# Routed rows that carry the gates of all eight experts

## The chip, the cores and the metric

The kernel runs on one core of one Trainium2 chip. The metric is the device time of one execution in microseconds, taken as the median of several runs. TensorE (PE) does the matrix products, VectorE (DVE), ScalarE (ACT) and GpSimd (POOL) the element-wise work; SyncE (SP), ACT and POOL have queues from which DMAs are issued.

## What is computed

A pre-norm transformer layer over x of 16 batches x 512 tokens x 256 features: banded attention with 16 heads, then a mixture of eight experts of which each token uses two.

```python
x = x + attention(layernorm(x))                  # banded softmax attention
gating = softmax(X @ Wg + bg)                    # X = layernorm(x), 8 gates for each token
top = argsort(gating)[..., -2:]                  # the two experts of each token
h = silu((X @ W1[e] + b1[e]) * (X @ W3[e] + b3[e]))
expert_out = h @ W2[e] + b2[e]
mixed = sum over the two experts of gating[e] * expert_out[e]
x = x + mixed @ Wf + bf                          # Wf is folded into W2 ahead of time
```

## The kernel before

The program has three parts, each a block that all engines leave before the next begins: a setup, the attention with the routing, and the experts.

**Attention and routing** (`build_attention`). A batch is 512 tokens, four tiles of 128. The work is a software pipeline of steps i = -1 to 17, each of 16 rounds n; the order on every engine is written out by hand, and step i holds rounds of attention of batch i, projections of batch i+3, the second norm of batch i-1, and the choice of experts of batch i-2. In each round PE writes scores for a maximum into `p_max`, DVE reduces them (L977), and PE's next scores wait for that.

For batch b the routing goes as follows. DVE normalises x2 to `x2n` (L930), ACT writes its high half into the row tile `rows[b % 3]` (`high_rows`, L829), POOL the low half (`low_rows`, L728). A row is 2 x 256 fp16 words and META = 6 words: token number, first gate, second gate, two words each (L41 to L45). DVE forms the eight gates (`softmax_gates`, L1031 to L1037), takes the largest and its expert, lowers that gate by 2 in place and takes the next (`choose`, L1039 to L1057); `place` (L1059 to L1075) turns PE's running counts into row numbers `slots`. POOL's `note(b)` (L684 to L693) copies the token number and the two gates into the row's words. POOL's `scatter(b, j)` (L695 to L707) sends the four tiles of rows to the regions of their j-th experts in the DRAM tensor `routed`, four indirect DMAs for j = 0 and four for j = 1. An expert reads one gate, the first of the row: so between the two sets POOL waits until the four DMAs of the first set have read the rows, and copies the second gate over the first (L699 to L704).

The order on POOL in a step is: `split_qk(i+2, 3)`, `low_rows(i-2)`, in even steps `all_magnitudes` (L712), in odd steps `low_weights(..., 2)` (L716), `scatter(i-3, 0)`, `split_qk(i+3, 0)` (L682), `second_norm` (L670), `note(i-2)`, `residual_bias` (L720), `split_qk(i+3, 1)`, `norm(i+4)`, `split_qk(i+3, 2)`, `scatter(i-3, 1)`, and in even steps `low_weights(..., 0)` and `(..., 1)`. For the last three batches (PROMPT = 13) both sets of batch i-2 go out at the end of step i, one behind the other. POOL leaves the block when all scatters have landed. SP meanwhile fills the end of the first expert's region (`fill`, L170) once DVE has the table of counts (`expert_tables`, L1077).

**Experts** (`build_experts`). For each expert a loop over tiles of 256 routed rows: SP loads the rows transposed (L1465), DVE copies them into place (L1579), PE does 48 matmuls of `hidden` and 24 of `result` (L1491, L1503), ACT loads the rows' words (`load_words`, L1539), and in `weighted` (L1541 to L1548) copies the token numbers and scales the result by the gate; POOL adds the scaled rows into `out` by an indirect DMA (L1628). In this trace there are 68 tiles.

Of the kernel before, what the change touches and what calls it, by code (L numbers as in the profile page):

```python
# [37 lines left out]
KC = HID // P  # L38
TOKENS = B * S
REGION = TOKENS + FILL  # L40
META = 6  # L41

M_TOKEN, M_GATE, M_SECOND = 0, 2, 4
USED = 4
ROW = 2 * D + META  # L45
NOWHERE = 1 << 20
NEG = -1e30
# [425 lines left out]
def build_attention(nc, io, keep):  # L473
    with ExitStack() as ctx:  # L474
# [31 lines left out]
        mv2 = sb("mv2", [P, NT, 2])  # L506
        rs2, var2 = sb("rs2", [P, NT]), sb("var2", [P, NT])
        lg, ge, gates = sb("lg", [P, NT, NE]), sb("ge", [P, NT, NE]), sb("gates", [P, NT, NE])
        gm, gs = sb("gm", [P, NT]), sb("gs", [P, NT])
        gw = [sb(f"gw{j}", [P, NT]) for j in range(TOPK)]  # L510
        one = [sb(f"one{j}", [P, NT, NE]) for j in range(TOPK)]
# [154 lines left out]
        @block.gpsimd  # L666
        def _(pool):
            def rstd(var, rs):

                return nc.gpsimd.tensor_tensor(rs[:], var[:], keep["neg_half"][:], ALU.pow)  # L670

            def norm(b):
                pool.wait_ge(s_mv1, b + 1)
                wait(pool, s_xn, b)
                rstd(var1, rs1)
                pool.drain()
                nc.gpsimd.tensor_tensor(shift1[:], less1[:], rs1[:], ALU.mult).then_inc(s_rs1, 1)

            def split_qk(b, k):

                taken(pool, s_free, "QK", b, k)
                nc.gpsimd.tensor_tensor(qk_lo[:, k, :], qf[:, k, :], qk_hi[:, k, :], ALU.subtract).then_inc(s_qk, 1)  # L682

            def note(b):  # L684

                words = rows[b % 3][:, :, 2 * D:ROW]
                pool.wait_ge(s_ch, b + 1)
                nc.gpsimd.tensor_copy(words[:, :, M_TOKEN:M_TOKEN + 2].bitcast(I32)[:, :, 0], keep["token"][:])
                nc.gpsimd.tensor_copy(words[:, :, M_GATE:M_GATE + 2].bitcast(F32)[:, :, 0], gw[0][:])
                nc.gpsimd.tensor_copy(words[:, :, M_SECOND:M_SECOND + 2].bitcast(F32)[:, :, 0], gw[1][:]).then_inc(s_noted, 1)  # L690
                pool.drain()
                nc.gpsimd.tensor_scalar(keep["token"][:], keep["token"][:], float(S), 0.0, ALU.add, ALU.add)
                pool.drain()  # L693

            def scatter(b, j):  # L695

                if j == 0:
                    pool.wait_ge(s_placed, b + 1)
                if j:  # L699
                    words = rows[b % 3][:, :, 2 * D:ROW]  # L700
                    pool.wait_ge(s_scat[b % 3], 128 * (b // 3) + 64)
                    nc.gpsimd.tensor_copy(words[:, :, M_GATE:M_GATE + 2].bitcast(F32)[:, :, 0],
                                          words[:, :, M_SECOND:M_SECOND + 2].bitcast(F32)[:, :, 0])
                    pool.drain()  # L704
                for t in range(NT):
                    nc.gpsimd.indirect_dma_start(out=io["routed"], out_offset=bass.IndirectOffsetOnAxis(  # L706
                        ap=slots[b % 3][:, j, t:t + 1], axis=0), in_=rows[b % 3][:, t, :].bitcast(U16), in_offset=None).then_inc(s_scat[b % 3], 16)  # L707

            def all_magnitudes(e):

                pool.wait_ge(s_wsum, e + 1)
                nc.gpsimd.tensor_tensor(w_all[:], w_sum[:], keep["half"][:], ALU.pow).then_inc(s_wall, 1)  # L712

            def low_weights(e, k):
                pool.wait_ge(s_whi, 3 * e + k + 1)
                nc.gpsimd.tensor_tensor(w_lo[:, k, :], w_mat[:, k, :], w_hi[:, k, :], ALU.subtract).then_inc(s_wlo, 1)  # L716

            def residual_bias(b):
                pool.wait_ge(s_xn, b + 1)
                nc.gpsimd.tensor_tensor(xt[b % HELD][:], xt[b % HELD][:], keep["bfc_row"][:, None, :].to_broadcast([P, NT, D]), ALU.add).then_inc(s_res, 1)  # L720

            def second_norm(b):
                pool.wait_ge(s_mv2, b + 1)
                rstd(var2, rs2).then_inc(s_rs2, 1)

            def low_rows(b):
                pool.wait_ge(s_hi2, b + 1)
                nc.gpsimd.tensor_tensor(rows[b % 3][:, :, D:2 * D], x2n[:], rows[b % 3][:, :, 0:D], ALU.subtract).then_inc(s_lo2, 1)  # L728

            for b in range(LEAD_BATCHES):  # L730
                norm(b)
                for k in range(4):
                    split_qk(b, k)
            norm(2)
            for i in STEPS:
                if exists(i + 2) and i > FIRST_STEP:
                    split_qk(i + 2, 3)
                if exists(i - 2):
                    low_rows(i - 2)
                if split_expert(i) is not None:  # L740
                    all_magnitudes(split_expert(i))
                if stored_expert(i) is not None:
                    low_weights(stored_expert(i), 2)
                if exists(i - 3) and i - 3 < PROMPT:
                    scatter(i - 3, 0)
                if exists(i + 3):
                    split_qk(i + 3, 0)
                if exists(i - 1):
                    second_norm(i - 1)
                if exists(i - 2):  # L750
                    note(i - 2)
                if exists(i):
                    residual_bias(i)
                if exists(i + 3):
                    split_qk(i + 3, 1)
                if exists(i + 4):
                    norm(i + 4)
                if exists(i + 3):
                    split_qk(i + 3, 2)
                if exists(i - 3) and i - 3 < PROMPT:  # L760
                    scatter(i - 3, 1)
                if exists(i - 2) and i - 2 >= PROMPT:
                    for j in range(TOPK):
                        scatter(i - 2, j)
                if split_expert(i) is not None:
                    low_weights(split_expert(i), 0)
                    low_weights(split_expert(i), 1)
            for p in range(3):
                pool.wait_ge(s_scat[p], 16 * TOPK * NT * len(range(p, B, 3)))
# [142 lines left out]
        def _(dve):  # L912
# [118 lines left out]
            def softmax_gates(b):  # L1031
                dve.wait_ge(s_ge, b + 1)
                nc.vector.tensor_reduce(out=gs[:], in_=ge[:], axis=AX.X, op=ALU.add)
                dve.drain()
                nc.vector.reciprocal(gs[:], gs[:])
                dve.drain()
                nc.vector.tensor_tensor(gates[:], ge[:], over_experts(gs), ALU.mult)  # L1037

            def choose(b, j):  # L1039

                dve.drain()
                if j == 0:
                    wait(dve, s_noted, b)
                nc.vector.tensor_reduce(out=gw[j][:], in_=gates[:], axis=AX.X, op=ALU.max)
                dve.drain()
                nc.vector.tensor_tensor(one[j][:], gates[:], over_experts(gw[j]), ALU.is_ge)
                dve.drain()
                nc.vector.tensor_tensor(pick[:], one[j][:], keep["expert_row"][:, None, :].to_broadcast([P, NT, NE]), ALU.mult)
                dve.drain()
# [2 lines left out]
                nc.vector.tensor_tensor(one[j][:], pick[:], over_experts(first[j]), ALU.is_equal)  # L1052
                dve.drain()
                if j == 0:
                    nc.vector.scalar_tensor_tensor(gates[:], one[0][:], -2.0, gates[:], ALU.mult, ALU.add)
                else:
                    nc.vector.tensor_tensor(chosen[:], one[0][:], one[1][:], ALU.add).then_inc(s_ch, 1)  # L1057

# [339 lines left out]
def build_experts(nc, io, kept):  # L1398
    with ExitStack() as ctx:
# [127 lines left out]
        def _(act):  # L1527
# [10 lines left out]
                after(act, s_yw, NB * g)  # L1538
                act.dma_start(words[:], io["routed"][bass.ds(at, FT), 2 * D:2 * D + USED].rearrange("(b p) r -> p b r", p=P)).then_inc(s_words, 16)  # L1539

            def weighted(g):  # L1541
                act.wait_ge(s_words, 16 * g + 16)
                act.wait_ge(s_y, g + 1)
                for b in range(NB):
                    after(act, s_sc[b], 16 * g)
                    nc.scalar.activation(tokens[:, b, :], words[:, b, M_TOKEN:M_TOKEN + 2], ACT.Copy)
                    nc.scalar.activation(yw[:, b, :], y[:, b, :], ACT.Copy,  # L1547
                                         scale=words[:, b, M_GATE:M_GATE + 2].bitcast(F32)).then_inc(s_yw, 1)  # L1548

            def body(e, p, at):  # L1550
                g = 0 if p is None else p + 1
                first_factor(e, g, 0)
                first_factor(e, g, 1)
# [4 lines left out]
                first_factor(e, g, 3)  # L1558
                silu(g, 1)
                if p is not None:  # L1560
                    weighted(p)

            at = None
            for e in range(NE):
                body(e, load_last(act, e - 1) if e else None, at)
                count, first = load_count(act, e), load_first(act, e)
                with act.Fori(0, count - 1) as j:
                    body(e, first + j, e * REGION + j * FT)
                at = e * REGION + count * FT - FT
            last_tile = load_last(act, NE - 1)  # L1570
            load_words(at, last_tile)
            weighted(last_tile)

        @block.vector
        def _(dve):
# [133 lines left out]
```

## Time and profile before

| | |
|---|---|
| median of 3 runs | 1512.9 us (1511.43 to 1518.19) |
| the profiled execution | 1508.1 us, span 1506.3 us |
| busy share PE, DVE, ACT, POOL | 84%, 64%, 53%, 43% |
| mean TensorE clock granted in it | 0.898 of full speed |
| setup | 0 to about 68 us, DVE's first norm statistics |
| attention and routing | to 949.8 us |
| experts | from there to the end |

A timeline row has the start and the length in microseconds, the engine, the line, the operation and its operands, and in brackets how long the engine had sat idle before it and what ended that. A row of several instructions that lie close together has their number as xN. "issue" means that the engine waited for nothing that the profile shows.

### The profile page before, as it was taken

What the parts mean: (1) busy time and instruction counts of PE and PEld (TensorE: products, weight loads), DVE (VectorE), ACT (ScalarE), POOL (GpSimd) and SP (SyncE); (2) the same over time, 40 slices, a digit from 0 to 9 for tenths busy, and PEclk for the clock granted to TensorE, in tenths of its full rate; (3) what the DMA queues carried; (4) which work ended last, traced back from release to release, by engine and by line L of the source; (5) the groups of instructions that cost most, each with busy time, mean ns of one, the idle gap of its engine ahead of it and who ended that gap; (6) DMA issues with size and microseconds to landing.
All of it is one profiled execution on the core that took longest, in us unless ns stands there. A gap on an engine that the chain in (4) does not pass through costs nothing. (4 is left out here: it accounts for less than half of the span.)

```text
span 1506.3 us, 46512 instructions
## 1 busy us (share of the span) xinstructions
PE 1270.5 (84%) x18200; PEld 930.1 (62%) x18200; DVE 968.7 (64%) x2064; ACT 798.4 (53%) x1388; POOL 647.7 (43%) x682
## 2 busy tenths in 40 slices
PE   6667888888788878887887773699999999999996
PEld 5534455554445545544555442588888888888885
DVE  4224668777776686778756656366666666666664
ACT  1344756666456655664554530355555555555554
POOL 2031422535345435354543645254455545544445
PEclk9867998998888888989987765799999999999999
DMA  6455464654545545545463232446654475464543
GB/s 130 166 130 145 99 188 102 174 128 127 161 127 142 149 105 173 132 122 162 113 171 98 88 99 85 106 66 122 126 113 66 66 175 69 64 123 67 66 64 48
DMA packets 226026, 175.35 MB, mean 116 GB/s; under 512 B 129082, under 2 KB 193082, under 8 KB 225866
## 3 DMA queue, kind: packets, MB, share of 16 engines
q1 hardware_dynamic: 167050, 116.62, 31.5%
q0 software_dynamic: 25728, 33.78, 13.0%
q10 hardware_dynamic: 33088, 22.71, 5.7%
q8 instruction: 114, 1.87, 0.6%
q14 instruction: 46, 0.38, 0.1%
HBM read 66.32 MB, written 89.40 MB: 103 GB/s over the span
## 5 line engine op out<-in xcount | busy, mean ns | idle before, releaser
L977 DVE TENSOR_REDUCE mx<-p_max 128x4 f32<-128x736 f32 (+1 forms) x256 | 219.1, 856 | 183.5 <-PE p_max L1248 179.2
L811 ACT ACTIVATE probs<-p_exp,unscale 128x736 f32<-128x736 f32 (+1 forms) x256 | 210.1, 821 | 206.3 <-PE p_exp L1248 204.4
L1491 PE MATMUL p_h<-xt_parts,w_hi 128*128 128x256 f16 x1824 | 273.7, 273 | 1.9 <-DVE xt_parts L1579 1.9
L1583 DVE SCALAR_TENSOR_TENSOR t<-p_h,b,t 128x256 f32<-128x256 f32 x272 | 131.0, 484 | 159.0 <-ACT t L1530 155.0
L1628 POOL DMA_INDIRECT out<-yw,tokens x136 | 211.9, 1558 | 28.3 <-POOL tick L1627 18.4
L1530 ACT ACTIVATE t<-p_h,b,undo 128x256 f32<-128x256 f32 x272 | 149.0, 559 | 91.8 <-PE p_h L1491 86.1
L1627 POOL TENSOR_TENSOR tick<-tick 128x1 f32<-128x1 f32 x136 | 82.9, 610 | 265.5 <-ACT yw L1547 265.5
L1491 PEld LDWEIGHTS p_h<-xt_parts,w_hi 128*128 128x128 f16 x1824 | 178.3, 98 | 22.7 <-DVE t L1583 2.1
L1491 PE MATMUL p_h<-xt_parts,w_lo 128*128 128x256 f16 x912 | 174.0, 273 | 0.0
L1241 PE MATMUL p_max<-mask,ident_bf 64*64 64x368 bf16 (+1 forms) x1024 | 93.8, 356 | 89.3 <-DVE mx L977 87.7
L706 POOL DMA_INDIRECT routed<-rows,slots x128 | 128.9, 1007 | 47.7 <-issue 47.7
L1279 PE MATMUL p_out<-probs,v 64*32 64x184 f32 (+1 forms) x4096 | 145.4, 345 | 1.3 <-DVE out_t L987 1.3
L682 POOL TENSOR_TENSOR qk_lo<-qf,qk_hi 128x512 f16<-128x512 f32 x64 | 74.2, 1159 | 150.8 <-ACT qk_hi L795 150.3
L1241 PEld LDWEIGHTS p_max<-mask,ident_bf 64*64 64x64 bf16 x1024 | 30.0, 107 | 163.1 <-DVE mx L977 113.2
L1535 ACT ACTIVATE hf<-t 128x512 f32<-128x512 f32 x136 | 85.7, 630 | 77.6 <-DVE t L1583 77.6
L1503 PE MATMUL p_y<-w_hi,h_hi 128*128 128x256 f16 x456 | 124.3, 273 | 1.2 <-DVE y L1598 1.2
L1503 PE MATMUL p_y<-w_hi,h_lo 128*128 128x256 f16 x456 | 124.3, 273 | 0.0
L1503 PE MATMUL p_y<-w_lo,h_hi 128*128 128x256 f16 x456 | 124.3, 273 | 0.0
L670 POOL TENSOR_TENSOR rs<-var,neg_half 128x4 f32<-128x4 f32 x32 | 33.0, 1032 | 195.1 <-DVE var L941 116.3
L1241 PE MATMUL p_exp<-mask,ident_bf 64*64 64x368 bf16 (+1 forms) x1024 | 89.8, 341 | 25.7 <-ACT probs L811 24.5
L1592 DVE SCALAR_TENSOR_TENSOR h_lo<-hf,h_scale,h_hi 128x512 f16<-128x512 f32 x136 | 102.2, 752 | 10.2
L793 ACT ACTIVATE qf<-p_sh,qk_bias,unscale 128x512 f32<-128x512 f32 x64 | 49.7, 777 | 88.8 <-PE p_sh L1216 88.8
(240 smaller groups left out, 2697.9 us busy)
## 6 DMA issues: line engine op xcount, KB each, us to landing
qk_dram<-qk_hi SPq DMA_DIRECT2D x128, 128.0 KB, 2.6
qs<-qk_dram SPq DMA_DIRECT2D x64, 192.0 KB, 4.2
ks<-qk_dram SPq DMA_DIRECT2D x64, 192.0 KB, 4.7
x_in<-in_x SPq DMA_DIRECT2D x64, 128.0 KB, 3.2
qk_dram<-qk_lo SPq DMA_DIRECT2D x64, 128.0 KB, 2.7
w_mat<-in_W ACTq DMA_DIRECT2D x32, 256.0 KB, 4.4
out<-x_sb SPq DMA_DIRECT2D x64, 128.0 KB
w_split<-w_first_hi SPq DMA_DIRECT2D x24, 256.0 KB
```

The source lines that it names most:

```text
L706: nc.gpsimd.indirect_dma_start(out=io["routed"], out_offset=bass.IndirectOffsetOnAxis(ap=slots[b % 3][:, j, t:t + 1], axis=0), in_=rows[b ...
L811: nc.scalar.activation(probs[r % 3][:, :, 0:hi - lo].rearrange("p (e s) w -> p e s w", e=2), p_exp[:, :, 0:2 * WIN].rearrange("p e (s w) - ...
L977: nc.vector.tensor_reduce(out=maxes, in_=p_max[:, :, 0:2 * WIN].rearrange("p e (s w) -> p e s w", s=2)[:, :, :, 0:hi - lo], axis=AX.X, op= ...
L1241: nc.tensor.matmul(out, keep["ident_bf"][Q * e:Q * e + Q, Q * e:Q * e + Q], keep["mask"][Q * e:Q * e + Q, None, off:off + hi - lo].to_broa ...
L1279: last = nc.tensor.matmul(p_out[32 * g:32 * g + 32, half, lo:hi], v[b % 3][rows_of, k, 4 * gk + g, :], probs[r % 3][rows_of, g, 0:hi - lo] ...
L1491: last = nc.tensor.matmul(p_h[:, m % KC, k, :], w[e][a][:, k, HID * c + P * m:HID * c + P * m + P], xt[:, x, c, :], start=(n == 0 and c == ...
L1503: last = nc.tensor.matmul(p_y[:, b, :], h[a][:, m, P * b:P * b + P], w[e][v][:, 2, D * m:D * m + D], start=(m == 0 and n == 0 and b % 2 == ...
L1530: nc.scalar.activation(t1[m][:], p_h[:, m % KC, 0, :], ACT.Identity, bias=kept["b13"][:, 0, e, m:m + 1], scale=kept["undo"][:, e:e + 1]).t ...
L1535: nc.scalar.activation(hf[q][:], t3[q][:], ACT.Silu).then_inc(s_silu, 1)
L1583: nc.vector.scalar_tensor_tensor(t3[m // 2][:, m % 2, :], p_h[:, m % KC, 1, :], kept["b13"][:, 1, e, m:m + 1], t1[m][:], ALU.add, ALU.mult ...
L1592: nc.vector.scalar_tensor_tensor(h[1][:, 2 * q:2 * q + 2, :], hf[q][:], kept["h_scale"][:, e:e + 1], h[0][:, 2 * q:2 * q + 2, :], ALU.mult ...
L1628: nc.gpsimd.indirect_dma_start(out=io["out"].rearrange("b s d -> (b s) d"), out_offset=bass.IndirectOffsetOnAxis(ap=tokens[:, b, :].bitcas ...
```

## The change

Rows get META = 18 words: the token number and the eight gates, two words each. `note` copies all eight gates with one instruction in place of two copies; the copy between the two sets, the wait before it and the drain behind it are gone. The experts read all 18 words of a row (36 bytes for 8), and `weighted` takes the gate of its own expert. `choose` lowers the largest gate in a new tile `others`, so that `gates` stays whole, and DVE's wait for the earlier `note` is now ahead of the instruction that writes `gates`.

```diff
-META = 6
-
-M_TOKEN, M_GATE, M_SECOND = 0, 2, 4
-USED = 4
+META = 2 + 2 * 8
+
+M_TOKEN, M_GATES = 0, 2
+USED = META
...
+        others = sb("others", [P, NT, NE])
...
                 nc.gpsimd.tensor_copy(words[:, :, M_TOKEN:M_TOKEN + 2].bitcast(I32)[:, :, 0], keep["token"][:])
-                nc.gpsimd.tensor_copy(words[:, :, M_GATE:M_GATE + 2].bitcast(F32)[:, :, 0], gw[0][:])
-                nc.gpsimd.tensor_copy(words[:, :, M_SECOND:M_SECOND + 2].bitcast(F32)[:, :, 0], gw[1][:]).then_inc(s_noted, 1)
+                nc.gpsimd.tensor_copy(words[:, :, M_GATES:META].bitcast(F32), gates[:]).then_inc(s_noted, 1)
...
-                if j:
-                    words = rows[b % 3][:, :, 2 * D:ROW]
-                    pool.wait_ge(s_scat[b % 3], 128 * (b // 3) + 64)
-                    nc.gpsimd.tensor_copy(words[:, :, M_GATE:M_GATE + 2].bitcast(F32)[:, :, 0],
-                                          words[:, :, M_SECOND:M_SECOND + 2].bitcast(F32)[:, :, 0])
-                    pool.drain()
...
+                wait(dve, s_noted, b)
                 nc.vector.tensor_tensor(gates[:], ge[:], over_experts(gs), ALU.mult)
...
+                left = (gates, others)[j]
                 dve.drain()
-                if j == 0:
-                    wait(dve, s_noted, b)
-                nc.vector.tensor_reduce(out=gw[j][:], in_=gates[:], axis=AX.X, op=ALU.max)
+                nc.vector.tensor_reduce(out=gw[j][:], in_=left[:], axis=AX.X, op=ALU.max)
...
-                    nc.vector.scalar_tensor_tensor(gates[:], one[0][:], -2.0, gates[:], ALU.mult, ALU.add)
+                    nc.vector.scalar_tensor_tensor(others[:], one[0][:], -2.0, gates[:], ALU.mult, ALU.add)
...
                     nc.scalar.activation(yw[:, b, :], y[:, b, :], ACT.Copy,
-                                         scale=words[:, b, M_GATE:M_GATE + 2].bitcast(F32)).then_inc(s_yw, 1)
+                                         scale=words[:, b, M_GATES + 2 * e:M_GATES + 2 * e + 2].bitcast(F32)).then_inc(s_yw, 1)
```

The rest of the diff hands `weighted` the number of the expert whose tile it finishes.

## Rows read from the trace of the kernel before

**Rows 1.** Windows, experts: length, busy PE, PEld, DVE, ACT, POOL (count), PEclk, DMA share, GB/s.

```profile
953.90:1494.00 540.10, 535.66 (x4884) 478.51 (x4885) 358.58 (x679) 303.49 (x677) 252.35 (x265) 1.00 0.55 91
```

**Rows 2.** Timeline of POOL, end of step 4 and start of step 5.

```profile
362.31 1.16 POOL L682 TENSOR_TENSOR qk_lo<-qf,qk_hi 128x512 f16<-128x512 f32 x1
363.42 0.19 POOL L702 COPY rows<-rows 128x4 f32<-128x4 f32 x1
364.41 1.13 POOL L706 DMA_INDIRECT routed<-rows,slots  x1 [0.80 <-issue]
...
376.69 2.11 POOL L716 TENSOR_TENSOR w_first_lo<-w_mat,w_first_hi 128x1024 f16<-128x1024 f32 x1
378.96 0.98 POOL L706 DMA_INDIRECT routed<-rows,slots  x1 [0.16 <-issue]
```

**Rows 3.** Timeline of DVE: the gates of steps 5 and 13.

```profile
375.67 3.18 DVE L1037 TENSOR_TENSOR gates<-ge,gs 128x32 f32<-128x32 f32 x1
...
774.83 1.88 DVE L1037 TENSOR_TENSOR gates<-ge,gs 128x32 f32<-128x32 f32 x1
```

**Rows 4.** Timeline of PE, first matmul after the gates of step 5.

```profile
381.70 0.42 PE L1241 MATMUL p_max<-mask,ident_bf 64*64 64x248 bf16 x4 [4.33 <-DVE mx L977]
```

**Rows 5.** Windows behind that gap (columns as Rows 1).

```profile
381.50:383.00 1.50, 1.30 (x32) 0.90 (x40) 1.26 (x5) 0.01 (x1) 1.18 (x2) 0.50 0.79 215
...
387.50:389.00 1.50, 1.50 (x41) 0.92 (x41) 0.94 (x2) 0.51 (x1) 0.00 (x0) 0.79 0.01 4
```

**Rows 6.** Timeline of ACT: the last operand that POOL's run needs.

```profile
369.11 0.77 ACT L795 ACTIVATE qk_hi<-p_sh,qk_bias,unscale 128x512 f16<-128x512 f32 x1
```

**Rows 7.** Timeline of POOL, last scatters of batches 13 to 15.

```profile
901.18 0.19 POOL L702 COPY rows<-rows 128x4 f32<-128x4 f32 x1 [5.31 <-DMA routed<-rows,slots]
...
914.14 1.04 POOL L670 TENSOR_TENSOR rs<-var,neg_half 128x4 f32<-128x4 f32 x1 [4.46 <-DVE var L926]
...
924.51 0.19 POOL L702 COPY rows<-rows 128x4 f32<-128x4 f32 x1 [1.66 <-DMA routed<-rows,slots]
...
930.62 2.07 POOL L728 TENSOR_TENSOR rows<-x2n,rows 128x1024 f16<-128x1024 f32 x1
...
934.65 1.07 POOL L706 DMA_INDIRECT routed<-rows,slots  x1 [0.81 <-issue]
...
941.41 0.19 POOL L702 COPY rows<-rows 128x4 f32<-128x4 f32 x1 [1.89 <-DMA routed<-rows,slots]
942.72 0.98 POOL L706 DMA_INDIRECT routed<-rows,slots  x1 [1.12 <-issue]
...
946.54 0.96 POOL L706 DMA_INDIRECT routed<-rows,slots  x1 [0.30 <-issue]
```

**Rows 8.** Timeline of SP: the first fill, and the first DMA of the experts.

```profile
937.23 0.36 SPq L170 DMA_DIRECT2D routed<-fill_rows  x1
949.82 0.32 SPq L1464 DMA_DIRECT2D opener<-routed  x1
```

**Rows 9.** The page, DMA issues: KB each, us to landing.

```profile
routed<-fill_rows SPq DMA_DIRECT2D x8, 518.0 KB, 3.6
```

**Rows 10.** Timeline of DVE beside the last scatters.

```profile
902.30 0.19 DVE L1037 TENSOR_TENSOR gates<-ge,gs 128x32 f32<-128x32 f32 x1
...
927.92 0.19 DVE L1057 TENSOR_TENSOR chosen<-one 128x32 bf16<-128x32 f32 x1
...
929.74 0.17 DVE L1075 CAST slots<-slot 128x8 int32<-128x8 f32 x1
930.04 2.67 DVE L1083 TENSOR_TENSOR fill_f<-runs,region_row 128x8 f32<-128x8 f32 x1
```

**Rows 11.** Timeline of the experts: the first tile's words, from issue to use.

```profile
965.82 0.41 ACTq L1539 DMA_DIRECT2D words<-routed  x1
...
971.91 0.20 ACT L1546 ACTIVATE tokens<-words 128x2 uint16<-128x2 uint16 x1 [1.30 <-DVE y L1598]
```

**Rows 12.** What ended ACT's idle time before it used words: us, times.

```profile
  DMA words<-routed: 12.4, 5
```

More of the change, by code:

```diff
@@ L1036, in softmax_gates @@
                 dve.drain()
+                wait(dve, s_noted, b)
                 nc.vector.tensor_tensor(gates[:], ge[:], over_experts(gs), ALU.mult)
             def choose(b, j):
+                left = (gates, others)[j]
                 dve.drain()
-                if j == 0:
-                    wait(dve, s_noted, b)
-                nc.vector.tensor_reduce(out=gw[j][:], in_=gates[:], axis=AX.X, op=ALU.max)
+                nc.vector.tensor_reduce(out=gw[j][:], in_=left[:], axis=AX.X, op=ALU.max)
                 dve.drain()
-                nc.vector.tensor_tensor(one[j][:], gates[:], over_experts(gw[j]), ALU.is_ge)
+                nc.vector.tensor_tensor(one[j][:], left[:], over_experts(gw[j]), ALU.is_ge)
                 dve.drain()
@@ L1539, in load_words, with weighted @@
                 act.dma_start(words[:], io["routed"][bass.ds(at, FT), 2 * D:2 * D + USED].rearrange("(b p) r -> p b r", p=P)).then_inc(s_words, 16)
-            def weighted(g):
+            def weighted(e, g):
                 act.wait_ge(s_words, 16 * g + 16)
@@ L1547, in weighted, with body @@
                     nc.scalar.activation(yw[:, b, :], y[:, b, :], ACT.Copy,
-                                         scale=words[:, b, M_GATE:M_GATE + 2].bitcast(F32)).then_inc(s_yw, 1)
-            def body(e, p, at):
+                                         scale=words[:, b, M_GATES + 2 * e:M_GATES + 2 * e + 2].bitcast(F32)).then_inc(s_yw, 1)
+            def body(e, p, before, at):
                 g = 0 if p is None else p + 1
@@ L1560, in body @@
                 if p is not None:
-                    weighted(p)
+                    weighted(before, p)
             at = None
             for e in range(NE):
-                body(e, load_last(act, e - 1) if e else None, at)
+                body(e, load_last(act, e - 1) if e else None, e - 1, at)
                 count, first = load_count(act, e), load_first(act, e)
                 with act.Fori(0, count - 1) as j:
-                    body(e, first + j, e * REGION + j * FT)
+                    body(e, first + j, e, e * REGION + j * FT)
                 at = e * REGION + count * FT - FT
@@ L1571, in _ @@
             load_words(at, last_tile)
-            weighted(last_tile)
+            weighted(NE - 1, last_tile)
         @block.vector
```

## The prediction

> **What bounds the kernel now.** I first asked what each part is limited by. In the experts PE is busy 535.66 of 540.10 us [rows 1]: a tile costs 540.10 / 68 = 7.9 us of matmuls, and at most 4.4 us in all could be won by better feeding. So the change gains there next to nothing, and can only lose. What it takes away lies on POOL, ahead of 949.8 us, and POOL is busy for 43% of the span. Such an engine matters only where another waits for it, so I went through POOL's timeline for stretches without idle time that end in something late, and found two kinds.
>
> The first kind is in the steady state. In step 4 POOL copies the second gates at 363.42, drains, and starts the four scatters at 364.41. Then it runs on without idle time through three low halves of weights, one `split_qk` and one `low_rows`, until 378.80 [rows 2]. DVE comes to the gates of step 5 at 375.67, an instruction that takes 0.19 us elsewhere [rows 10], and is held for 3.18 us, to 378.85 [rows 3]: exactly the end of POOL's run. Behind the gates stands the next maximum, and PE waits for that 4.33 us [rows 4]; ACT has nothing either. All engines stand still for the end of a POOL run. The same picture comes five times, in steps 5, 7, 9, 11 and 13; the first (3.18 us) and the last (1.88 us) are shown. PE pays twice: behind such a gap its granted clock is 0.50, 1.2 GHz in place of 2.4, and it comes back only some 6 us later [rows 5].
>
> The second kind is the end of the routing. From 914.14, where DVE's last variance sets it free, POOL works through everything that is left, to its last scatter at 946.54 + 0.96 = 947.50; the experts begin at 949.82 [rows 7, 8]. Nobody else is busy at the end, so each us off POOL there is a us off the time.
>
> **The change, part by part.** *Copy and drain between the sets, batches 0 to 12.* Here the wait is free, since the first set landed long before. The instruction ahead of the copy ends at 362.31 + 1.16 = 363.47, the first scatter starts at 364.41 and takes 1.13 us. Without copy and drain a scatter stands directly behind an element-wise instruction, and such a one starts 0.16 us after its end and takes 0.98 [rows 2]. So the first starts at 363.63, 0.78 us earlier, and is 0.15 us shorter: 0.93 us. POOL's run starts and ends so much earlier only if its operands are there. The last that it needs is high QK, done by ACT at 369.11 + 0.77 = 369.88 [rows 6]; POOL took it ahead of `low_rows` (2.07 us, as in rows 7) and of the row at 376.69: 376.69 - 2.07 - 1.16 = 373.5, and would take it at 372.5. So the run ends at 377.87, DVE's gates, due at 375.67 as before, are held 2.25 us, and the standstill is 0.93 us shorter. Five times: 4.65 us. The last one keeps the whole too, as 1.88 is more than 0.93. In the other steps a wait for ACT stands behind the scatters and absorbs it. Low bound 0 (if other work of DVE or PE turns out late), high bound 5 x 0.99 = 5 us (copy start to scatter start), and more with the clock (rival below).
>
> *Wait, copy and drain, batches 13 to 15.* Batch 13: the wait is 5.31 us long, but POOL then idles 4.46 us for DVE at 914.14 [rows 7]; all of it is gained on POOL and waited off there: 0. One thing moves: the sets of batches 12 and 13 end at 901.18 - 5.31 - 0.93 = 894.94, the next at 894.94 + 0.30 + 4 x 0.96 + 3 x 0.30 = 899.98, and `low_rows(14)` would run from there to 902.05, just ahead of DVE's gates at 902.30 [rows 10]. Were they to meet, DVE's last attention output would be up to 0.6 us later. I take 0. Batch 14: 1.66 + 0.19 + 1.12 (the gap behind the copy, as at 942.72) = 2.97 us between the sets against 0.30 between scatters of one set: 2.67 us less. But POOL's `low_rows(15)` then starts at 927.9 in place of 930.62. That is where DVE writes `chosen` (927.92) [rows 10]; in the trace before it met DVE at 930.04, where an instruction on 8 columns was held for 2.67 us, off the path. Held to 930.0, `chosen` is 1.9 to 2.0 us late, and `slots`, done at 929.91, come at about 931.8. POOL itself would be ready for the first scatter of batch 15 at 934.65 - 2.67 = 932.0. I let it start at 932.3: 2.35 us saved here. Batch 15: 1.89 + 0.19 + 1.12 = 3.20 against 0.30, 2.90 us, with nothing behind it but the landing, 2.1 us as before. Sum for the end: 5.25 us; bounds 4.2 (both meetings with DVE, with half a us to spare) and 5.6 (none).
>
> What is late next: SP's fill of the first region, issued at 937.23 [rows 8], lands 3.6 us later [rows 9], at about 941. POOL's end would be at 947.50 - 5.25 + 2.1 = 944.4. The fill has 3 us to spare, so it does not take over.
>
> *The note.* Three copies become two, one of them 32 columns wide and not 4. A POOL copy of 4 columns is 0.19 us [rows 2]; `low_rows` takes 2.07 us for 1024 columns [rows 7], 2 ns a column, so 28 columns more are 0.06 us. Net between -0.1 and +0.1 us a batch: 0.
>
> *DVE.* `others` in place of `gates` is an instruction of the same shape. The wait for `note(b-1)` stands three instructions earlier, with the gates, all of `choose` and DVE's later maxima behind it. `note(b-1)` is done in the middle of the step before. It is tightest for batch 15: `note(14)` is over before the four scatters that end at 924.51 - 1.66 = 922.85, five us of issue earlier, so by 918, and the gates are thirteen short instructions ahead of `chosen` at 927.92, at about 924: 0. POOL would have to be 6 us late before it cost anything.
>
> *Longer rows.* Scatters and fills move 1060 bytes a row for 1036, 2.3% more. A scatter's time on POOL is that of its 128 row numbers; I take none for the bytes. Bound: 2.3% of 0.96 us x 128 is 2.8 us of POOL time, of which the eight scatters at the end are 0.2 us. The transposed load reads 1024 bytes a row as before, at another pitch.
>
> *Words.* ACT reads 36 bytes for 8 of each of 256 rows. The rows show only the old size: issued at 965.82, used at 971.91 and then the wait was for DVE's result, not for the words [rows 11]. So the landing has up to 6.1 us. At five tiles, behind an expert's weights in the DMA queues, words were the last to come, for 12.4 us in all [rows 12], and PE still lost at most 4.4 us in the whole part [rows 1]. Bounds for the change: 0 (a row is one small piece either way) and, if all five waits grew in the ratio of the bytes, 12.4 x 3.5 = 43 us on ACT, part of it on PE. I take 0, as the number of pieces, 256, does not change. The Trainium skill (DMA: Bandwidth & Descriptors, How a descriptor splits into AXI transactions) counts 32-byte beats and has a read start at the 256-byte boundary below it. By that rule an estimate is some 4 to 5 beats for 8 bytes and one more for 36, a quarter more and not 4.5 times; the sum stays.
>
> *The lock.* Why DVE is held, and how long, decides the first term. The rows say: to the end of POOL's whole run, over three of its instructions [rows 2, 3]. The Trainium skill (SBUF — State Buffer, Who interferes with whom) has a DVE instruction with two SBUF inputs wait for one GpSimd instruction that reads SBUF. By that alone the hold of step 5 would have been 1.0 us, not 3.18; the trace does not agree, but a shift of the run gives the same 0.93 us by either.
>
> **Sum.** 4.65 + 5.25 = 9.9 us. The profiled execution took 1508.1 us (span 1506.3), so 1498.2. It lies 4.8 us under the median of the three runs, 1512.9; from that the change gives 1503.0, a gain of 0.65%. Half a per cent, about what a measurement of this kernel can tell from no change, is 7.6 us: the border is 1505.3.
>
> **The rivals.**
>
> *A, the forecast*: both terms. 1500.5 to 1506.5. For it: PE, ACT and DVE really stand still together. Chance 0.48; three quarters of it lie over the border.
>
> *B, the clock gives back more.* The gap of 4.33 us on PE becomes 3.4, and if TensorE then stays at 2.4 GHz, up to 6 us at half speed become 3: up to 3 us more, five times. For it: the gap is what the clock falls behind. Against: that 3.4 us is still long. With two to five of five kept: 6 to 15 us more, 1488 to 1497. Chance 0.18.
>
> *C, only the end is gained.* The 0.93 us come back as another wait a few rounds on, for instance of DVE in a POOL instruction that it used to miss (such holds are 1.88 to 3.18 us [rows 3, 10]). Then 1512.9 - 5.25 = 1507.7. Chance 0.20.
>
> *D, nothing.* POOL's indirect DMAs, now twelve and sixteen in a row, run into a full queue, or longer rows cost at the end what the waits did: 1511 to 1514. For it: at 895.87 the eight outstanding ones needed 5.31 us to be read [rows 7], though weights were loading then; in the last two waits four needed only 1.66 and 1.89. Chance 0.07.
>
> *E, slower, the words.* If the wider words land later than 6.1 us behind their issue, ACT's scaling and its next `first_factor` are late in every tile, and PE, which has no idle time, pays 68 times. To eat the 9.9 us and 7.6 more takes 0.26 us a tile; at 0.4 us it is 27 - 10 = 17 us more, 1530. For it: five waits of up to 2.6 us already. Against: the slack in all other tiles. Chance 0.07.
>
> **How the numbers follow.** Faster by over 0.5%: 0.75 x 0.48 + 0.18 + a little of C = 0.56. Slower: E, 0.06. The rest, 0.38, is within. The range leaves out most of E and the far end of B: 1494 to 1512.
>
> **What would show it.** Right: no row for L702; the gates of steps 5 to 13 held about 2.25 us (0.95 in the last); PE's gaps behind them 3.4 us; eight scatters 1.27 us apart at the end, for batch 15 from about 932.3 less the 4.65 us gained earlier; the experts beginning some 9.9 us earlier, at 940; and as long as before. Wrong: the holds unchanged or DVE held at new places (C); a full clock behind the gaps (B); gaps of over 0.3 us between scatters or a longer landing (D); ACT's waits for words in many more than five tiles (E).

## The result, and the profile after

Before: 1511.5 us median of 20 runs (1501.3 to 1518.2). After: 1504.7 us of 20 runs (1498.3 to 1512.0). The ratio is 0.996, 95% interval 0.9943 to 0.9977: 6.0 us less, between 3.5 and 8.6 (the medians differ by 6.8). The forecast was 1503.0 us in a range of 1494 to 1512, 9.9 us less. The direction holds, the gain is smaller: 0.4%, so within the half per cent that the text set as its border.

The two profiled executions hardly differ as wholes: 1507.3 us with a span of 1505.5 after, 1508.1 and 1506.3 before. Whoever looked only there would find nothing. So the trace is read in three stretches: up to DVE's last variance, from there to the last scatter, and the experts. All lines of the changed kernel from 700 on are 5 or 6 lower than before.

**Steady state.** POOL's timeline of the changed kernel, end of step 4 and start of step 5 (start, length, engine, line, operation, what it wrote and read, idle time and its releaser), answers to [rows 2]:

```profile
361.44 1.16 POOL L683 TENSOR_TENSOR qk_lo<-qf,qk_hi 128x512 f16<-128x512 f32 x1
362.77 1.13 POOL L700 DMA_INDIRECT routed<-rows,slots  x1 [0.17 <-issue]
...
375.06 2.12 POOL L710 TENSOR_TENSOR w_first_lo<-w_mat,w_first_hi 128x1024 f16<-128x1024 f32 x1
377.34 0.99 POOL L700 DMA_INDIRECT routed<-rows,slots  x1 [0.16 <-issue]
```

The copy is gone, and the scatter starts 0.17 us behind the element-wise instruction. But it still takes 1.13 us. From the start of the first row here to the end of POOL's run are 377.18 - 361.44 = 15.74 us, before 378.80 - 362.31 = 16.49: 0.75 us less, where 0.93 was forecast.

DVE's gates of steps 5 and 13, the first matmul of PE behind those of step 5, and the window behind its gap (length, busy PE, PEld, DVE, ACT, POOL with counts, granted clock, DMA share, GB/s), for [rows 3], [rows 4] and [rows 5]:

```profile
374.32 2.90 DVE L1032 TENSOR_TENSOR gates<-ge,gs 128x32 f32<-128x32 f32 x1
...
775.37 0.85 DVE L1032 TENSOR_TENSOR gates<-ge,gs 128x32 f32<-128x32 f32 x1
```

```profile
380.07 0.42 PE L1235 MATMUL p_max<-mask,ident_bf 64*64 64x248 bf16 x4 [4.05 <-DVE mx L971]
```

```profile
380.30:381.80 1.50, 1.50 (x40) 0.78 (x32) 1.11 (x6) 0.43 (x1) 1.20 (x2) 0.50 0.76 226
...
386.30:387.80 1.50, 1.50 (x32) 0.99 (x25) 1.27 (x2) 0.87 (x1) 0.00 (x0) 1.00 0.00 0
```

The gates end at 377.22, POOL's run at 377.18: DVE is still held exactly to the end of the run. All five holds are shorter: 2.90, 2.94, 2.33, 2.55 and 0.85 us, 11.6 in all, where before had 3.18, 3.64, 3.28, 3.33 and 1.88, 15.3 in all. PE's gaps behind them are 4.05, 4.09, 3.47, 3.70 and 2.76 us, and the granted clock behind all five is still half (0.50 or 0.51).

The hold of step 5 itself is only 0.28 us shorter, although POOL's run ends 0.75 us sooner. DVE also came sooner: 374.32 - 361.44 = 12.88 us behind the start of `split_qk`, before 375.67 - 362.31 = 13.36. How long a hold is depends on both ends, so a shorter hold isn't yet as much time won.

In the even steps the forecast let a wait for ACT absorb the gain. It does: the first `split_qk` of step 6 waits 1.32 us for ACT, before 0.57.

```profile
418.84 1.16 POOL L683 TENSOR_TENSOR qk_lo<-qf,qk_hi 128x512 f16<-128x512 f32 x1 [1.32 <-ACT qk_hi L789]
```

**The end of the routing.** POOL, for [rows 7]:

```profile
897.57 2.07 POOL L722 TENSOR_TENSOR rows<-x2n,rows 128x1024 f16<-128x1024 f32 x1
912.59 1.05 POOL L671 TENSOR_TENSOR rs<-var,neg_half 128x4 f32<-128x4 f32 x1 [12.95 <-DVE var L920]
...
916.16 1.26 POOL L700 DMA_INDIRECT routed<-rows,slots  x1 [0.80 <-issue]
...
921.54 0.96 POOL L700 DMA_INDIRECT routed<-rows,slots  x1 [0.31 <-issue]
...
926.33 2.08 POOL L722 TENSOR_TENSOR rows<-x2n,rows 128x1024 f16<-128x1024 f32 x1
928.80 0.19 POOL L689 CAST rows<-token 128x4 int32<-128x4 f32 x1 [0.39 <-DVE chosen L1051]
928.94 0.21 POOL L690 COPY rows<-gates 128x32 f32<-128x32 f32 x1
...
931.02 1.08 POOL L700 DMA_INDIRECT routed<-rows,slots  x1 [0.79 <-DVE slots L1069]
...
936.21 0.96 POOL L700 DMA_INDIRECT routed<-rows,slots  x1 [0.30 <-issue]
...
940.01 0.96 POOL L700 DMA_INDIRECT routed<-rows,slots  x1 [0.30 <-issue]
```

DVE beside it ([rows 10]), and SP ([rows 8]):

```profile
896.88 2.82 DVE L1023 TENSOR_TENSOR lg<-lg,gm 128x32 f32<-128x32 f32 x1
...
901.31 0.19 DVE L1032 TENSOR_TENSOR gates<-ge,gs 128x32 f32<-128x32 f32 x1
...
926.01 2.45 DVE L1046 TENSOR_TENSOR one<-pick,first 128x32 f32<-128x32 f32 x1
928.54 0.19 DVE L1051 TENSOR_TENSOR chosen<-one 128x32 bf16<-128x32 f32 x1
...
930.36 0.17 DVE L1069 CAST slots<-slot 128x8 int32<-128x8 f32 x1
```

```profile
935.35 0.36 SPq L170 DMA_DIRECT2D routed<-fill_rows  x1
...
943.67 0.33 SPq L1458 DMA_DIRECT2D opener<-routed  x1
```

Eight scatters now stand 1.27 us apart without a break. POOL's `low_rows(15)` moved forward, onto the instruction ahead of `chosen`, and held it for 2.45 us. So `slots` end at 930.53, and POOL waits 0.79 us for them. From where DVE's last variance sets POOL free (912.59 here, 914.14 before) the first scatter of batch 15 starts after 18.43 us, before after 20.51: 2.1 less; between its sets 2.9 us are gone. But from the end of the last scatter, 940.97, the experts begin after 2.70 us, where it was 2.32: 0.4 us more. Sum 4.6 us, forecast 5.25. This stretch, up to the experts' first DMA, repeats closely: 35.7 to 36.5 us in the seven profiles of this study that keep the wait and the copy in the last three batches, 31.0 to 31.4 in the seven that don't.

**The experts.** They begin 949.82 - 943.67 = 6.15 us earlier (4.6 of the end, 1.55 of the time before the last variance), and take 561.8 us in place of 556.5. This is the row of waits for words, as [rows 12]:

```profile
ACT tokens L1540 <- DMA words<-routed: 14.9, 5, 3.2
```

Five waits as before, 14.9 us for 12.4. Whether wider words or rows cost those 5 us, and whether the steady part paid at all, could not be read from two executions. That is what the runs are for.

### The profile page after: what moved, and what is told of

Its sections match the earlier page's. It is cut to its first block and busy times, and to the rows that moved or that the text cites. A ratio compares the mean times of both kernels' runs of the same rounds, so it can differ in the third digit from the quotient of the medians.

```text
span 1505.5 us, 46464 instructions
## 1 busy us (share of the span) xinstructions
PE 1279.7 (85%) x18200; PEld 933.4 (62%) x18200; DVE 963.2 (64%) x2064; ACT 798.1 (53%) x1388; POOL 642.4 (43%) x650
## 5 line engine op out<-in xcount | busy, mean ns | idle before, releaser
L1586 DVE SCALAR_TENSOR_TENSOR h_lo<-hf,h_scale,h_hi 128x512 f16<-128x512 f32 x136 | 102.2, 752 | 10.2
```

Source lines behind the costliest of these rows:

```text
L1586: nc.vector.scalar_tensor_tensor(h[1][:, 2 * q:2 * q + 2, :], hf[q][:], kept["h_scale"][:, e:e + 1], h[0][:, 2 * q:2 * q + 2, :], ALU.mult ...
```

## The experiments

The theory (A): both terms pay, wide rows and words cost nothing. The rivals: only the end pays (C), and the width costs part of it (D, E). "Before" is run beside each group on its chip: 1513.9 us with the first four, 1512.8 with the next four, 1511.2 with the two tens and `rows_moved`, 1516.6 with the last.

**no_replace.** The kernel before, with 6-word rows, without the `if j:` block. The second expert's rows carry the first gate.

```diff
-                if j:
...
-                    pool.drain()
```

> Rows of 6 words as before, but the wait, the copy and the drain between the two sets are left out, so that the second expert reads the first gate. If longer rows and words cost nothing, this is the change itself: ratio about 0.996 to the kernel before (6 us). If the wider rows cost some 4 us in the experts, as the profile after suggests (561.8 us from the experts' first DMA to the end, 556.5 before), this is 9 to 10 us faster, ratio 0.9935, and its experts take 556 to 557 us. If the steady part gives nothing, the experts begin about 5 to 6 us earlier and not 10.

1508.1 us, 0.9959 (0.9926 to 0.9992): as much as the whole change. Holds of the gates 10.0 us in all, from the end of DVE's last variance to the end of the last scatter 28.6 us (after 28.5, before 33.4), 2.9 us more to the experts, and these 562.0 us long, although rows and words are as narrow as before. So neither the longer experts nor the longer landing in the trace of after needs wider rows or words.

**long_rows, long_rows_words.** The width alone: rows of 18 words, 12 of them zero; the second also reads all 18.

```diff
-META = 6
+META = 18
...
-USED = 4
+USED = 18
...
+            for p in range(3):
+                nc.vector.memset(rows[p][:, :, 2 * D + 6:ROW], 0.0)
```

> Only the rows grow to 18 words (12 of them zeros), the replacement stays and ACT reads 4 words as before. Rows cost nothing: ratio 1.000. Rows are the cause of the longer experts: ratio 1.002 to 1.003.

> Rows of 18 words, and ACT reads all 18, with the replacement as before. Words cost nothing: the same as long_rows. Words are the cause: experts 3 to 5 us longer than in long_rows, ACT's waits for words above 12.4 us (14.9 in the profile after), ratio 1.002 to 1.003.

0.9983 (0.9957 to 1.001) and 0.9963 (0.993 to 0.9997). Neither is slower. ACT's waits for words are 13.9 and 16.0 us, five each, the experts 559.9 and 559.7 us long, holds and scatters as before. So D's longer rows and E's wider words cost nothing that could be measured here. That an edit which only adds bytes came out at 0.9963 has no cause that the trace shows, and it is a measure of what such a ratio is worth: some 5 us for one kernel against another. Neither kernel lacks the copy, so part of the 6.2 us of `no_replace`, measured beside them, may be of that kind too.

**after_again.** The changed kernel once more beside these.

> The changed kernel once more, for a second profile. If the 5.3 us longer experts belong to the change, they are seen again (560 to 562 us from the experts' first DMA); if they were that one execution's, the experts take 556 to 558 us. DVE's gates of steps 5 to 13 held 2.3 to 2.9 us, 0.9 in step 13.

1506.0 us, 0.9941 (0.9906 to 0.9976); against `long_rows_words` (1511.2 us), which has the same rows and words and still the copy, it is 5.2 us less. Holds 1.19, 2.39, 2.50, 2.75 and 0.88 us, the end again 28.46 us, the experts 558.1 us long. So the 561.8 us of the first profile belong to the execution. Over all profiles of this study the experts last 556.5 to 562.0 us, mean 559.2, with narrow words (8 kernels) and 558.1 to 562.1, mean 560.3, with wide ones (6): 1.1 us apart, within the spread.

**end_only, steady_only.** The replacement is left out for batches 13 to 15 alone, and for 0 to 12 alone. There the second expert's rows carry the first gate.

```diff
-                if j:
+                if j and b < PROMPT:
```

```diff
-                if j:
+                if j and b >= PROMPT:
```

> Rows of 6 words, the replacement left out for batches 13 to 15 alone (their second expert reads the first gate). From DVE's last variance to the last scatter 28.5 us as in the changed kernel, 33.4 before, so the experts begin 4.6 us earlier in that stretch; holds of the gates unchanged at 3.2 to 3.6. If the end is all that the change gains, ratio 0.997, the same as the changed kernel's 0.996; if the steady part gives its 4.65 us too, the changed kernel stays 3 to 4 us ahead of this one, which the intervals may just not tell.

> Rows of 6 words, the replacement left out for batches 0 to 12 (their second expert reads the first gate), the last three as before: the other half of end_only. On POOL 0.77 us a batch go. By the slope of ten_copies_odd (17.7 us for 5 x 2.9) the five odd batches give 0.77 x 5 x 1.2 = 4.6 us, by that of ten_copies_even (7 us for 7 x 2.9) the others 0.77 x 7 x 0.35 = 1.9 us: 6.5 us, ratio 0.9957. As forecast (0.93 x 5): 0.9969. If small gains are given back where large losses are paid: 0.999 to 1.000. From DVE's last variance to the last scatter 33.5 us as before; holds 0.8 us shorter than before.

| | ratio (95%) | five holds, us | last variance to last scatter, us |
|---|---|---|---|
| end_only | 0.9984 (0.9951 to 1.0016) | 15.2 | 28.6 |
| steady_only | 0.9975 (0.995 to 1.0001) | 9.7 | 33.6 |

The profile parts them at the end of the routing, and in the gates of steps 5 to 11: each has its own term and not the other's. DVE's gates of step 5, in `steady_only` without the replacement and in `end_only` with it:

```profile
375.76 2.66 DVE L1037 TENSOR_TENSOR gates<-ge,gs 128x32 f32<-128x32 f32 x1
```

```profile
376.73 3.09 DVE L1037 TENSOR_TENSOR gates<-ge,gs 128x32 f32<-128x32 f32 x1
```

In step 13 the gates of `steady_only` take 0.19 us, and those of `no_replace` too, but the hold isn't gone. It has moved to an earlier instruction of DVE, `lg`, which takes 0.19 us in that step before (in `steady_only` here; `no_replace` has 3.97 us):

```profile
771.31 3.94 DVE L1029 TENSOR_TENSOR lg<-lg,gm 128x32 f32<-128x32 f32 x1
```

By time the end gives 2.4 us and the steady part 3.8, each with an interval that includes no gain; together 6.2, and the whole change 6.0. Over eight profiles the five holds of the gates are 15.1 us in the mean with the copy and 10.2 without. That looks like 4.9 us won, but not all of it is. The table has the ten steps from DVE's gates of step 4 to those of step 14 in these profiles, all in us but the clock:

| | stretch | DVE in `gates`, `lg`, `x2n` | PE busy | granted clock |
|---|---|---|---|---|
| before | 496.3 | 47.6 | 409.5 | 0.88 |
| long_rows | 495.3 | 47.4 | 409.9 | 0.88 |
| long_rows_words | 489.7 | 45.7 | 407.2 | 0.88 |
| end_only | 492.0 | 46.8 | 411.0 | 0.87 |
| after | 495.4 | 42.1 | 417.5 | 0.86 |
| after_again | 494.5 | 42.8 | 417.0 | 0.87 |
| no_replace | 495.7 | 48.5 | 416.1 | 0.87 |
| steady_only | 499.1 | 49.9 | 417.8 | 0.86 |

In the two profiles of the changed kernel 4.4 us of held time are gone. In `no_replace` and `steady_only` they are back, at `lg` and `x2n`: that is rival C at work. And the stretch isn't shorter without the copy: 496.2 us in the mean, against 493.3 with it. The same matmuls (8149 to 8154) kept PE busy for 417 us and not 409, at a slightly lower clock, which in these profiles eats what the shorter gaps give. Whether the change does that isn't shown. Eight single executions are few, and over all executions the mean clock isn't lower without the copy (0.895 in the 20 of the changed kernel and the 12 of `after_again`, 0.893 in the 33 of before beside the latter). So the traces show the shorter holds and PE gaps of the changed kernel, but not that the steady part becomes shorter; for that there is only the 0.9975 of `steady_only`, whose interval ends at 1.0001.

**four_copies, ten_copies_odd, ten_copies_even.** The suspected cost, multiplied: copy and drain four times in batches 0 to 12, or ten times in the odd or the even ones of these.

```diff
-                    nc.gpsimd.tensor_copy(words[:, :, M_GATE:M_GATE + 2].bitcast(F32)[:, :, 0],
...
+                    for _ in range(10 if b < PROMPT and b % 2 == 1 else 1):
+                        nc.gpsimd.tensor_copy(words[:, :, M_GATE:M_GATE + 2].bitcast(F32)[:, :, 0],
```

> The kernel before, with the copy and drain between the two sets made four times in place of once for batches 0 to 12 (the end as before). Each repetition is some 0.95 us on POOL, 2.9 us a batch. If the time on POOL in the steady state is paid through DVE's held gates (forecast), the holds of steps 5 to 13 grow from 3.3 to about 6 us (1.8 to 4.7 in step 13), and the time by 5 x 2.9 = 14 us, ratio 1.009 to 1.010. If the steady part is given back by other waits (rival C), the holds grow but the time does not: ratio below 1.003.

> The kernel before, with the copy and drain made ten times for the odd batches up to 11, whose second set goes out in an even step, ahead of POOL's long run. A repetition measured 0.32 us in four_copies (1.15 us for four in place of 0.19 for one), so 9 more are 2.9 us a batch, and the holds of the gates in steps 5 to 13 grow from 3.3 to 6.2 us. If each us of hold is one us of time: +14.4 us, ratio 1.0095. If the clock behind the longer gaps is paid too: more, up to 1.015. If other waits give it back: 1.003 or less.

> The same for the even batches up to 12, whose second set goes out in an odd step, where POOL next waits for ACT by some 0.6 us. If only the holds of the gates cost time: holds unchanged at 3.3 us, ratio 1.000 to 1.002. If the 9.5 us of four_copies came from both halves alike: 1.007 or more.

`four_copies` was a weak lever: three more copies took only 0.96 us, a third of what was expected, as this row of its POOL timeline says (four copies, 1.15 us). 1.0063 (1.0033 to 1.0093), the first four holds 4.2 to 4.4 us.

```profile
363.83 1.15 POOL L703 COPY rows<-rows 128x4 f32<-128x4 f32 x4
```

`ten_copies_odd`: POOL, DVE and PE in steps 4 and 5.

```profile
364.09 3.08 POOL L703 COPY rows<-rows 128x4 f32<-128x4 f32 x10
...
380.23 2.11 POOL L717 TENSOR_TENSOR w_first_lo<-w_mat,w_first_hi 128x1024 f16<-128x1024 f32 x1
```

```profile
376.03 6.37 DVE L1038 TENSOR_TENSOR gates<-ge,gs 128x32 f32<-128x32 f32 x1
```

```profile
385.25 0.42 PE L1242 MATMUL p_max<-mask,ident_bf 64*64 64x248 bf16 x4 [7.48 <-DVE mx L978]
```

POOL's run ends at 382.34, the gates at 382.40. DVE arrives when it always does, and is held for whatever POOL has left; PE's gap grows from 4.33 to 7.48 us, ratio 1.0117 (1.0081 to 1.0154). The five holds grew by 30.6 - 15.3 = 15.3 us, the time by 17.7 us (12.2 to 23.3): about 1.2 us for each us of hold.

`ten_copies_even` puts the same 2.9 us where a wait for ACT follows. The five holds stayed (3.09, 3.32, 3.46, 3.53, 1.71); but the gates of steps 6 and 8, which took 0.19 us before, took 0.99 and 1.08, and it came out at 1.0046 (1.0018 to 1.0075), 7 us, where at most 1.002 was expected. POOL's timeline behind the scatters of step 5, first before, then here:

```profile
420.74 1.15 POOL L682 TENSOR_TENSOR qk_lo<-qf,qk_hi 128x512 f16<-128x512 f32 x1 [0.57 <-ACT qk_hi L795]
```

```profile
427.42 1.16 POOL L682 TENSOR_TENSOR qk_lo<-qf,qk_hi 128x512 f16<-128x512 f32 x1
```

The wait for ACT is only 0.57 us long, far less than nine copies. What is left over makes POOL later, and DVE meets it in even steps: `low_rows` from 428.53 holds the gates that DVE comes to at 429.68. That is 1.7 us of the 7; where the rest arises wasn't found. The change goes the other way: there POOL comes early, and a wait for ACT can take up any amount of that (the 1.32 us above). So this run says nothing on what the even batches gain, and the 1.9 us that the expectation of `steady_only` drew from it have no ground.

If each of the six odd batches hides a cost like that of an even one (1 us), the 1.2 falls to about 0.8. With the 4.5 us that the changed kernel's holds of the gates are shorter, the steady part would be worth 3.4 to 5.2 us: an estimate, if a gain is paid like a loss, which the table above doesn't bear out.

**weights_later, rows_moved, runs_moved.** If the holds are what costs, their rest can be had by moving POOL's work off the moment at which DVE writes the gates. All three start from the changed kernel: the third low half of weights goes behind the first set of scatters; or `low_rows` does; or both.

```diff
 # weights_later
-                if stored_expert(i) is not None:
-                    low_weights(stored_expert(i), 2)
...
+                if stored_expert(i) is not None:
+                    low_weights(stored_expert(i), 2)
 # rows_moved
-                if exists(i - 2):
+                if exists(i - 2) and i >= B:
...
+                if exists(i - 2) and i < B:
+                    pool.wait_ge(s_ch, i - 1)
+                    low_rows(i - 2)
```

> The changed kernel, with only the third low_weights moved behind the first scatters. By the lock the hold of the gates ends 2.1 us earlier, with the end of low_rows: 0.2 to 0.8 us left in place of 2.3 to 2.9. The moved instruction (2.1 us) then runs beside DVE's choose and holds one instruction of it for up to 2 us, behind which the next maximum stands: gain over the changed kernel between 0 and 9 us, I expect 3; ratio to before 0.994.

> The changed kernel with only low_rows moved behind the first scatters and the wait for DVE's chosen (steps up to 15); the third low_weights stays where it was, since in runs_moved ACT's load of the next expert's weights waited 8.5 us for it in each odd step. POOL's run ends 2.06 us earlier: holds of 0.4 to 0.9 us and none in step 13, and nothing of DVE with two SBUF inputs stands behind chosen. Expected 9 us faster than the changed kernel, ratio to before 0.989 to 0.990; if the holds are not worth their length, 0.994.

> The changed kernel, with low_rows and the third low_weights moved behind the first scatters and behind a wait for DVE's chosen, for the steps up to 15: POOL's run then ends before DVE's gates. Theory of the lock: gates take 0.19 us in all steps, PE's gaps of 3 to 4 us in steps 5 to 13 are gone, 11 us faster than the changed kernel, more if TensorE keeps 2.4 GHz behind the gates; ratio to the kernel before 0.989 or less. If the holds are not on the path, or the moved instructions hold DVE elsewhere: ratio 0.996 as the changed kernel.

| | ratio to before (95%) | us | holds of the gates, us |
|---|---|---|---|
| weights_later | 0.9949 (0.992 to 0.9978) | 1505.4 | 0.58, 0.70, 1.17, 0.47, 0.21 |
| rows_moved | 0.9924 (0.9889 to 0.9958) | 1501.9 | 0.74, 1.14, 0.48, 0.50, 0.19 |
| runs_moved | 1.0161 (1.0112 to 1.0209) | 1534.6 | 0.19 in all |

`weights_later` moves the hold and doesn't end it. Its POOL and DVE:

```profile
381.36 2.13 POOL L710 TENSOR_TENSOR w_first_lo<-w_mat,w_first_hi 128x1024 f16<-128x1024 f32 x1
```

```profile
380.99 2.57 DVE L1046 TENSOR_TENSOR one<-pick,first 128x32 f32<-128x32 f32 x1
```

`rows_moved` lets POOL wait until DVE has written `chosen`, and then runs `low_rows` beside instructions that aren't held. Its POOL and PE:

```profile
373.57 2.13 POOL L710 TENSOR_TENSOR w_first_lo<-w_mat,w_first_hi 128x1024 f16<-128x1024 f32 x1
...
383.61 2.06 POOL L722 TENSOR_TENSOR rows<-x2n,rows 128x1024 f16<-128x1024 f32 x1 [2.97 <-DVE chosen L1054]
```

```profile
378.60 0.30 PE L1238 MATMUL p_max<-mask,ident_bf 64*64 64x248 bf16 x4 [1.85 <-DVE mx L974]
```

PE's gap is 1.85 us in place of 4.05. Behind this one the granted clock stays at 1.00; behind the other four, of 1.63 to 2.29 us, it still fell to half, for 3 to 6 us. Its 0.9924 is the lowest ratio of all, though its interval reaches into that of the changed kernel. From the gates of step 4 to those of step 14 its profile takes 492.1 us with PE busy for 410.0 (`weights_later` 487.8 and 410.6), less than the four without the copy in the table above. `runs_moved` has no hold at all and is the slowest: `low_weights`, now behind the wait for `chosen`, runs at 398.60, and ACT, which needs the place, stands. There are six such waits, 49.5 us in all.

```profile
398.60 2.11 POOL L710 TENSOR_TENSOR w_first_lo<-w_mat,w_first_hi 128x1024 f16<-128x1024 f32 x1
```

```profile
ACT probs L808 <- POOL w_first_lo L710: 8.5, 1, 8.5
```

## Why the prediction was right, and where it was off

*The steady term, 5 x 0.93 = 4.65 us.* Right as far as the chain goes: DVE is held to the end of POOL's run, the run ends earlier, PE's gaps shrink. `ten_copies_odd` shows the same chain with a longer run, and there the time follows. Two things were off. The 0.93 was put too high: 0.78 us of it, the earlier start of the first scatter, came as forecast. The other 0.15 us, "shorter", did not: the scatter takes 1.13 us with or without a copy ahead of it. The sentence had generalised from one row, the first scatter of step 5 (0.98, [rows 2]), to another place. Five times 0.75 us is 3.8 us. And that the time falls by as much as the standstill of DVE isn't shown for the small step that the change makes. From the 6.0 us measured (3.5 to 8.6) the end takes 4.6; that leaves 1.4 us for all else, between 1.1 more time and 4.0 less, and the 4.65 us lie outside. By the repetition, 8.9 us (3.6 to 14.2), it would be 4.3, with a far wider interval. `steady_only` measured 3.8 us, with an interval from 7.6 to nothing, in executions of which the profiled one had its holds back at other instructions. The total came near to the forecast in part by luck: the three runs that it started from had a median 1.4 us above that of the 20, and the range, 1494 to 1512, holds even the 1511.5 us of the kernel before.

*The lock.* The hold of step 5 goes over two POOL instructions and not three: DVE comes at 375.67, in `low_rows` (374.66 to 376.71), and is let go behind the third low half (378.80). That one instruction would explain only 1.0 us stands, and `ten_copies_odd` (6.37 us, to the end of a longer run) bears it out.

*The end, 5.25 us.* The 2.90 us between the sets of batch 15 came to the digit. The 2.35 us at its first scatter were 2.1: `low_rows(15)` held DVE one instruction earlier than forecast, at `one` and not at `chosen`, and POOL's first scatter then waited for `slots`. The landing, "2.1 us as before", was the other mis-sized term: 2.3 us became 2.7, in every kernel whose last eight scatters have no pause between the sets (2.68 to 2.93), with narrow rows too (2.93, 2.79); with the pause it is 2.32 to 2.46 in all but `ten_copies_even` (2.66). 4.6 us in all, and this term is shown: from the last variance to the experts it is 31.0 to 31.4 us in all seven profiles without the pause, and 35.7 to 36.5 in all seven with it. By time `end_only` shows 2.4 us, with an interval from 7.4 less to 2.4 more, so the profile is the better witness. At batch 14 `low_rows(14)` didn't pass ahead of the gates: it started 2.4 us earlier than forecast and held DVE's `lg` at 896.88 for 2.82 us, which cost nothing that could be seen, as POOL then waited 12.95 us for DVE's variance (the variance itself came 1.55 us earlier than before).

*What was taken at nothing.* The note's wide copy is 0.21 us for 0.19. DVE's earlier wait never showed as idle time ahead of the gates. Rows and words: `long_rows` and `long_rows_words` aren't slower; the wider words make the waits some 2 us longer in all, which is nearly nothing and not nothing. The fill, issued at 935.35, is down by about 938.3 (a fill takes 2.9 us in this trace, the median of eight) and did not take over.

*Rival B* falls by the windows: the clock was half behind all five gaps of 2.76 to 4.09 us. In `rows_moved` it stayed full behind one gap of 1.85 us, but not behind gaps of 1.63 and 1.65, so these runs give no length of gap that keeps it. *Rival C* isn't excluded. In `no_replace` and `steady_only` holds of the gates came back at `lg` and `x2n`; in the changed kernel they did not (its `x2n` at 598.29, 2.97 us for four, was as long before, 2.98 at 603.70). Against C stand only `ten_copies_odd`, a step of other size and direction, and the 0.9975. *D* and *E* fall, but for the 0.4 us of landing.

*What stays open.* The corrected terms give 3.8 + 4.6 = 8.4 us; measured were 6.0 (3.5 to 8.6), and 8.9 (3.6 to 14.2) in the repetition. The end's 4.6 us are sure. How much of the steady 3.8 us arrives isn't: anything from nothing to all of it fits, and PE's 8 us of longer busy time in the four profiles without the copy have no known cause. Most of the 7 us of `ten_copies_even` is unexplained, and so is the 0.9963 of `long_rows_words`.

## What to carry to other kernels

When GpSimd does "free" work, look at which VectorE instruction it overlaps: one with an ideal time of 0.2 us that takes 3 is the sign, and what matters is where POOL's unbroken run ends, not which of its instructions is long. Taking a little off such a run gains that little at most; moving the run to where VectorE does other work may gain more (`rows_moved`), as long as nobody waits for what was moved (`runs_moved`). And for a change worth half a per cent, compare stage by stage over several profiles, as whole spans differed by more; but don't stop at the wait that was to shrink. Look whether the stage around it got shorter too, and whether the wait came back under another name, as `gates` did at `lg`.

## What was not expected of the hardware

- A VectorE instruction on two SBUF operands waited out up to 6.4 us of POOL's work, across several instructions of it ([rows 3] and `ten_copies_odd`). Neighbours that read PSUM, and reductions, went on at their usual length (`mx` 0.93 us and `gs` 0.17 us beside the run of [rows 2]).
- Ten POOL copies of 4 columns, each with a drain, take 3.08 us, 0.31 each, where one copy with its drain delayed the next scatter by 0.77 us: most of that price is paid once, ahead of the scatter.
- Eight scatters without a pause land 0.4 us later than two sets of four with a pause, whether a row has 1036 or 1060 bytes; one kernel with a pause (`ten_copies_even`, 2.66 us) has the longer landing too.
- Reading 36 bytes in place of 8 from each of 256 rows lengthened ACT's waits for words (five, four in `no_replace`): 15.5 us in the mean of six profiles in place of 13.3 in eight, so by some 2 us in all and far from 4.5 times; the time of the kernel doesn't show it.
